# Graph network and attention on one core: every engine's loops written out straight

## What is computed

```python
def pool_max(h, src, dst):                 # max over the incoming edges, 0 where there is none
    return where(count(dst) > 0, segment_max(h[src], dst, num_segments=N), 0)

def gnn(e):
    h1 = relu(e @ Wp1.T + bp1)
    x  = relu(concat([e, pool_max(h1)]) @ Wm1.T + bm1)
    y2 = relu(concat([x, pool_max(x)]) @ Wm2.T + bm2);  x = layernorm(y2 + x, g2, b2)
    y3 = relu(concat([x, pool_max(x)]) @ Wm3.T + bm3);  return layernorm(y3 + x, g3, b3)

def attention(h):                          # 8 heads of 32
    q, k, v = (h @ Wq + bq) * 32 ** -0.5, h @ Wk + bk, h @ Wv + bv
    s = einsum('edh,edh->eh', q[src], k[dst])
    e = exp(s - segment_max(s, src)[src]);  z = segment_sum(e, src)
    return segment_sum((e / z[src])[:, None, :] * v[dst], src).reshape(N, -1) @ Wo + bo

x = x + gnn(relu(layernorm(x)))
x = x + attention(relu(layernorm(x)))
```

## Time and profile before

| | |
|---|---|
| Median of three runs | 6380.84 us (6357.94 to 6386.19) |
| The profiled execution's own time | 6447.71 us |
| Its span | 6445.9 us |
| DVE, POOL busy | 62%, 61% of the span |
| TensorE's matmuls, ACT busy | 37%, 23% |
| Mean granted TensorE clock | 0.649 |
| Maximum passes 1, 2, 3 | 1267, 1366, 1249 us |
| Attention | 1792 us |

### The profile page before, as it was taken

One profiled execution on the slowest core, in us unless ns is written; L12 is line 12 of the kernel. 1 busy time (PEld: TensorE's weight loads), 2 busy tenths in 40 slices (PEclk: granted clock), 3 DMA queues, 4 the chain that ended last, 5 costly groups with the idle time before them and its releaser, 6 DMA issues. The chain is left out here.

```text
span 6445.9 us, 61988 instructions
## 1 busy us (share of the span) xinstructions
PE 2375.4 (37%) x12678; PEld 1454.0 (23%) x12738; DVE 4027.6 (62%) x8418; ACT 1480.9 (23%) x2309; POOL 3958.7 (61%) x3748
## 2 busy tenths in 40 slices
PE   3222210025556555656777766678100000000004
PEld 2111100014444444444333322245000000000003
DVE  4555556554555555557665655566577778788786
ACT  3000000002111212125666666654000000000001
POOL 1666577745555566655888888840566666666663
PEclk9555555557666666668888888889555555555557
DMA  4444444534444444445555555443555555556553
GB/s 132 166 170 152 147 166 169 175 129 150 140 153 155 153 156 163 169 146 167 172 171 175 179 168 169 163 131 119 168 178 173 175 176 176 175 178 184 171 170 97
DMA packets 339899, 1035.76 MB, mean 161 GB/s; under 512 B 73288, under 2 KB 140576, under 8 KB 306424
## 3 DMA queue, kind: packets, MB, share of 16 engines
q0 software_dynamic: 208656, 611.17, 32.4%
q1 hardware_dynamic: 131176, 423.86, 17.5%
HBM read 648.42 MB, written 386.47 MB: 161 GB/s over the span
## 5 line engine op out<-in xcount | busy, mean ns | idle before, releaser
L495 POOL DMA_INDIRECT G<-tab,ix x2349 | 2647.5, 1127 | 1177.1 <-issue 694.3
L517 DVE SCALAR_TENSOR_TENSOR G<-G,reset 128x256 f32<-128x256 f32 x2349 | 1128.1, 480 | 835.6 <-DMA G<-tab,ix 462.2
L1312 POOL DMA_INDIRECT kv<-kvtab,ix x936 | 884.8, 945 | 285.0 <-issue 285.0
L927 ACT ACTIVATE signs<-iota,off 128x937 bf16<-128x937 f32 x783 | 802.0, 1071 | 448.2 <-PE bank L941 325.1
L941 PE MATMUL trio<-signs,work 128*128 128x512 bf16 (+1 forms) x2289 | 722.2, 430 | 384.5 <-DVE work L913 369.6
L1432 PE MATMUL trio<-ident,state 128*128 128x128 f32 x2 | 0.7, 448 | 1799.2 <-DVEq L1452 1799.2
L1310 POOL DMA_INDIRECT q<-qtab,ix x234 | 221.0, 945 | 529.1 <-DVE ix L1320 429.1
L941 PEld LDWEIGHTS trio<-signs,work 128*128 128x128 bf16 x2349 | 232.9, 110 | 772.3 <-issue 417.7
L1432 PEld LDWEIGHTS trio<-ident,state 128*128 128x128 f32 x2 | 0.3, 204 | 1800.0 <-DVEq L1452 1800.0
L854 PE MATMUL wide<-next,lowT 128*128 128x49 f32 x1566 | 294.4, 315 | 153.5 <-issue 153.4
L854 PEld LDWEIGHTS wide<-next,lowT 128*128 128x128 f32 x1566 | 276.6, 230 | 185.9 <-issue 182.5
(11 more groups left out here) (307 smaller groups left out, 5784.8 us busy)
## 6 DMA issues: line engine op xcount, KB each, us to landing
hist<-G SPq DMA_DIRECT2D x261, 1152.0 KB
G<-tab,ix POOLq DMA_INDIRECT x2349
ahist<-state SPq DMA_DIRECT2D x78, 408.0 KB
tab<-o SPq DMA_DIRECT2D x147, 128.0 KB
kv<-kvtab,ix POOLq DMA_INDIRECT x936
h<-tab SPq DMA_DIRECT2D x98, 128.0 KB
cur<-tab SPq DMA_DIRECT2D x98, 128.0 KB
kvtab<-okv SPq DMA_DIRECT2D x49, 256.0 KB
```

Of the source, the lines that this page charges most:

```text
L495: g.indirect_dma_start(G[b][:, k, :], None, tab, bass.IndirectOffsetOnAxis(ix[:, b, k:k + 1], 0)).then_inc(s_eg[b].sem, 16)
L517: ins = v.scalar_tensor_tensor(out=G[b][:, k, :], in0=before, scalar=reset[:, bass.ds(n * J + k, 1)], in1=G[b][:, k, :], op0=ALU.add, op1= ...
L927: a.activation(self.signs[:, r, :], self.iota[:, :], ACT.Sign, bias=self.off[:, bass.ds((i * UB + b) * J + k, 1)]).then_inc(self.signs_mad ...
L1312: g.indirect_dma_start(kvs[b][:, k, :], None, kvtab, bass.IndirectOffsetOnAxis(ix[:, b, k:k + 1], 0)).then_inc(s_eg[b].sem, 16)
```

## The change

`staged` loses the loop: each turn is issued with its number as a constant, for all engines. `Chain` loses `body` and `term`, since every value is a constant, and the callers lose the arguments that gave the links of a turn. Stages, delays, buffers and semaphores stay. The jumps between the program's blocks stay as well.

```diff
@@ class Chain
     def __init__(self, eng, sem):
-        self.eng, self.sem, self.base, self.term = eng, sem, 0, 0
+        self.eng, self.sem, self.base = eng, sem, 0
...
     def inc(self, ins):
         ins.then_inc(self.sem, 1)
         self.base += 1
-        return self.base + self.term
+        return self.base
...
-    @contextmanager
-    def body(self, i, per, times):
-
-        start, self.term = self.base, i * per
-        yield
-        assert self.base - start == per, (self.base - start, per)
-        self.base, self.term = start + per * times, 0
...
-def staged(eng, steps, un, stages, chain=None, links=0):
+def staged(eng, steps, un, stages):
...
-    def filled(t):
-
-        have = [sum(0 <= t * un + u - delay < count for u in range(un)) for delay, _, count in stages]
-        return have if all(n in (0, un) for n in have) else None
-
-
-    first = 1 + -(-max(delay for delay, _, _ in stages) // un)
-    t = 0
-    while t < turns:
-        end = t + 1
-        while t >= first and filled(t) and end < turns and filled(end) == filled(t):
-            end += 1
-        if end == t + 1:
-            turn(t, lambda delay, count, u: 0 <= t * un + u - delay < count)
-        else:
-            with eng.Fori(t, end) as i:
-                with chain.body(i - t, links * un, end - t) if chain else nullcontext():
-                    turn(i, lambda delay, count, u: 0 <= t * un + u - delay < count)
-        t = end
+    for t in range(turns):
+        turn(t, lambda delay, count, u: 0 <= t * un + u - delay < count)
...
-                    staged(v, NB, UB, stages, chain, J - 1 + side.links)
+                    staged(v, NB, UB, stages)
...
-                    staged(v, NBA, UB, [(0, score), (1, carry_on), (0, weigh)], chain, 4 + R + 3 * R + 6)
+                    staged(v, NBA, UB, [(0, score), (1, carry_on), (0, weigh)])
```

More of the change, by code:

```diff
@@ L15 @@
-from contextlib import ExitStack, contextmanager, nullcontext
+from contextlib import ExitStack
 import concourse.bass as bass
@@ L416, in _ @@
                         stages.append((3, first, 1))
-                    staged(v, NT, UN, stages, chain, 2 + per_out)
+                    staged(v, NT, UN, stages)
                 @blk.scalar
@@ L1200, in _ @@
                         stages += nodes.vector(v)
-                    staged(v, NT, UN, stages, chain, residual * 3)
+                    staged(v, NT, UN, stages)
                     if nodes:
@@ L1525, in join @@
                         v.tensor_tensor(o[:, u, :], o[:, u, :], X[:, i * UN + u, :], ALU.add).then_inc(c_out.sem, 1)
-                    staged(v, NT, UN, [(0, place_ix(v, node_ix2)), (3, divide), (7, join)], chain, 2)
+                    staged(v, NT, UN, [(0, place_ix(v, node_ix2)), (3, divide), (7, join)])
                 @blk.scalar
```

## The result

| | before | changed |
|---|---|---|
| Median of four runs | 6383.51 us | 6154.83 us (6118.47 to 6193.82) |
| Ratio, 95% interval | 1 | 0.9647 [0.9573, 0.972] |
| Profiled execution, its span | 6447.71, 6445.9 us | 6118.47, 6116.7 us |

The change makes the kernel faster by 3.5%, 229 us between the medians. A second measurement, on another chip beside the experiments, gave 0.9678 [0.9638, 0.9719].

A forecast was written before the change was run, and what follows sets the result against it. No engine is full, so waits bound the kernel: DVE leads the attention, POOL bounds pass 3. Attention -33, passes 1 and 2 -15, pass 3 0, short stages -5 sum to -53 us: 6328 us median, range 6225 to 6440.

The forecast's parts named there:

- the attention's mechanism: Attention, DVE: shorter links in a batch and turn-arounds save 0 to 66 us over 24 looped turns; middle taken, -33 us.
- the price of links: Attention, DVE: links between dependent instructions cost more in a loop, three taking 0.97 us against 0.75 straight; 0.62 us a batch.
- Passes 1 and 2, DVE: Maximum passes 1 and 2: faster folds save at most 77 us, mostly lost in longer waits; -15 us.
- its shrinking by hundreds of us: Sign of a wrong step: a pass moves most, above all if late semaphores shrink or grow by hundreds of us.
- pass 3, 0: Third maximum pass: POOL is the bound without free time and covers what DVE, ACT and TensorE save; 0 us.
- The short stages: Combines, projections and finish: turn-arounds save between 0 and 10 us; -5 us taken.
- Nothing gained: Rival, chance 0.33: late answers and POOL's bursts set the turn, so only short stages give; 6376 us.
- Everything counts: Rival, chance 0.12: DVE is on the path throughout the attention and all savings count, 153 us; 6229 us.
- Code becomes a wait: Rival, chance 0.17: DVE and POOL stop while straight code is loaded, some 81 packets more; 6424 to 6458 us.
- price of a branch: Attention turn ends: about 108 ns a compare-and-branch, so 24 turn ends worth 2.6 us; not used in the forecast.
- my row: Attention, DVE: a trace row showing the whole turn-around costs 0.69 us more in the loop, 16.6 us over 24 turns.

The follow-up runs named there:

- register links: The changed kernel, but DVE counts its links in a register again in the maximum passes and the attention; 0.9717 of the kernel before.
- e1: The kernel before with only DVE's program written straight, in every stage; 0.9847 of the kernel before.
- e7: The kernel before with only POOL's program written straight; 0.9947 of the kernel before.
- the hold: Two lines in `gather` that keep POOL one batch nearer to DVE; everywhere in the changed kernel 0.9626, in the kernel before 0.9872.
- e12: The changed kernel with POOL held one batch nearer to DVE in the maximum passes and the attention; 0.9626 of the kernel before.
- e14: The changed kernel with POOL held in maximum pass 1 and the attention alone; 6072.64 us, 0.9479 of the kernel before.
- double turns: The kernel before with loops kept on all engines, but two turns in a loop's body; 0.9973 of the kernel before.

## Why the prediction was right or wrong

*Right: the attention's mechanism.* I took 33 us out of 0 to 66; the attention alone gave 45 (29 to 63 by its interval). The batch of 18.5 us came, DVE's short idle times fell by 48 us, and the late answers did not fall (213 us before, 218 and 262 in two profiles of the changed kernel).

*Right in effect, wrong in name: the gaps.* I called them the price of links. The register links show that they come with operands that have register addresses. The sum was not touched by that, since both went.

*Wrong, and the step that failed: "Passes 1 and 2, DVE", -15 us of at most 77.* Only folds were priced, and the late semaphores of the earlier trace rows were taken as a cover that swallows what DVE saves: "folds that are done sooner make that wait longer". The runs show the contrary: the three passes alone gave 155 us. In the pair of profiles before and changed, DVE's own gaps gave 29 and 17 us in passes 1 and 2 (its idle times under 0.6 us fell from 41 to 12 and from 30 to 13), within the 77; but the late answers fell by 183 and 136 us, of which the waits for gathers took back 135 and 34. That is the part that no term had. A wait that is 700 us long in a profile was set down as fixed without asking what makes it long; the prediction itself had named its shrinking by hundreds of us as the sign of this error.

*Wrong by a little: pass 3, 0.* It lost some 25 us in both profiles of the changed kernel. POOL stayed the bound; what fell is the time that its gathers are busy, which I had taken as fixed: 996 to 972 us. It is about 986 with DVE alone straight (e1) and 997 with POOL alone straight (e7); why is open. The short stages gave about 23 by the barriers, where I had 5 of at most 10: mostly combine 1 and the finish.

*The rivals.* "Nothing gained" fell with the verdict. "Everything counts", 6229 us, came nearest, by counting folds and turn-arounds at their full price; its price for the passes was 77, not 155, and it too had no term for what the late answers gave there. "Code becomes a wait" fell: its packets came as counted, but no stop is seen that goes with them. A gap of 1.20 us like that of the earlier trace rows comes nine times in the attention of the changed kernel, at uneven distances, and four times in its second profile; with the hold, which loads as much code, none is left in e12 and one in e14 (others of 0.4 to 0.5 us stay, four and nine). What the Trainium skill says in "Runtime: NRT & Kernel Launch", section Instruction fetch mechanics, that the crossing is mostly hidden, agrees with these 248 packets and no stop beside them.

By the Trainium skill's price of a branch, "Advanced Engine Details and Errata", section Control Flow Timing, turn ends were to be worth less than by my row. The double turns took 67 of DVE's 134 branches away, with those of the other engines, and gave 17 us (3 to 31), where 67 times the 0.69 us of my row are 46: not all of a turn-around counts, if it is as long everywhere as in the attention. At the page's price 67 branches are 7 us, an estimate; the measured interval holds that too.

*Open:* by which way a loop on any engine makes answers late more often, and what on the chip keeps an answer of TensorE back for 20 us while POOL gathers. The runs show only on what it depends. The hold shortens POOL's bursts and the row of transfers that they start alike, so it does not tell which of the two holds answers back; the wait above ended 3.8 us after the last gather of the burst.

## What to carry to other kernels

A long idle time that is put down to another engine's late answer is a quantity to be explained, not a cover: find out what it hangs on before letting it swallow a gain. Where engines feed each other in a ring through several buffers, small delays on every engine can count together, and the one that runs ahead can harm the others: hold it, stage by stage, and measure. Written-out loops cost code, and here no time that goes with it showed.

## What was not expected of the hardware

DVE stood up to 23.8 us at one wait for an answer of TensorE that was done, while GpSimd issued gathers without a pause until some 5 us before the wait's end; holding GpSimd one batch nearer brought the waits at that line from 74.4 to 8.1 us in sum. DVE's wait on its own semaphore was late as well (6.04 us in the row above). On DVE an instruction with an operand at a register address came about 0.1 us later (three in 0.97 us against 0.75); a semaphore value in a register alone cost no gap.
